# Three edge loops of a four-layer graph network: a PSUM ring of four, and two operations a group later

## What is computed

```
h = relu(layernorm(x));  x += attention over all edges, messages added at the row (layer 0)
h = relu(layernorm(x));  x += edge network (layer 1):
    e    = relu(concat(h[src], edge_attr) @ W1a + b1a) @ W1b + b1b
    agg  = segment_sum(e, dst) / count;   out = relu(concat(h, agg, u) @ W2a + b2a) @ W2b + b2b
h = relu(layernorm(x));  x += GATv2 (layer 2), 4 heads of 64, then 1 head of 128:
    m    = xl[src] + xr[dst] + w_edge * We;   logit = sum(leaky_relu(m) * att)
    out  = segment_sum(segment_softmax(logit) * xl[src], dst)
h = relu(layernorm(x));  x += three EdgeConv steps (layer 3):
    h    = relu([x_i, x_j - x_i] @ W1 + b1) @ W2 + b2;   out = segment_max(h, dst)
```

## Time and profile before

| What | us |
|---|---|
| median of three runs | 12301.65 |
| lowest and highest of them | 12288.66 and 12314.6 |
| the profiled execution, its time | 12306.0 |
| the profiled execution, its span | 12304.2 |

### The profile page before, as it was taken

The page is one execution under the profiler, slowest core; times in us unless marked ns, Lnnn a source line. Parts: engine busy times, 40 slices in busy tenths (PEclk is TensorE's granted clock), DMA queues, the critical chain, the costliest instruction groups (busy, mean ns, idle before and its releaser), DMA issues. The chain is left out here.

```text
span 12304.2 us, 181472 instructions
## 1 busy us (share of the span) xinstructions
PE 7391.4 (60%) x39114; PEld 6245.1 (51%) x39115; DVE 7065.6 (57%) x13587; ACT 2531.9 (21%) x8694; POOL 6720.9 (55%) x6703
## 2 busy tenths in 40 slices
PE   4944444366665677636444443637777677767776
PEld 4944444355554555524344443635555555555554
DVE  6844444433345888866754545675555555555555
ACT  2500000011110000046400000322333233323332
POOL 0088888366642666523236664316666466646665
PEclk7966666555557888879867666768898888888888
DMA  4356556322213666545324443313333334433433
GB/s 118 72 95 96 96 96 97 88 65 65 66 51 93 210 211 213 192 99 157 104 83 127 131 129 103 113 47 129 131 131 132 110 133 132 132 109 132 132 130 121
DMA packets 828886, 1436.26 MB, mean 117 GB/s; under 512 B 183440, under 2 KB 494844, under 8 KB 788336
## 3 DMA queue, kind: packets, MB, share of 16 engines
q1 hardware_dynamic: 531712, 981.94, 25.6%
q0 software_dynamic: 297072, 453.23, 16.7%
HBM read 1115.44 MB, written 320.07 MB: 117 GB/s over the span
## 5 line engine op out<-in xcount | busy, mean ns | idle before, releaser
L1612 POOL DMA_INDIRECT T<-gather_d,srci x2508 | 2516.5, 1003 | 1604.1 <-issue 652.4
L1198 PE MATMUL PS<-T 128*128 x3328 | 1045.0, 404 | 1072.3 <-DVE T L1214 824.1
L838 POOL DMA_INDIRECT added_d<-T,slots x832 | 1292.1, 1553 | 288.4 <-issue 224.1
L920 DVE TENSOR_TENSOR T<-T,PS 128x128 f32 (+1 forms) x2092 | 560.3, 287 | 1465.4 <-remote 1064.7
L1198 PEld LDWEIGHTS PS<-T 128*128 128x128 f32 x3328 | 710.6, 244 | 1223.1 <-issue 1169.7
L1149 POOL DMA_INDIRECT T<-wide_d,srci x832 | 832.6, 1001 | 738.4 <-PEq L71 287.1
L1149 POOL DMA_INDIRECT T<-gather_d,srci x832 | 825.6, 992 | 677.4 <-PEq L71 239.5
L943 POOL DMA_INDIRECT T<-gather_d,srci x832 | 799.8, 961 | 643.3 <-DVE T L1014 265.5
L1731 DVE TENSOR_TENSOR_SCAN T<-T,PS 128x512 f32<-128x512 f32 x624 | 798.1, 1279 | 597.7 <-remote 362.9
L1420 PE MATMUL PS<-T 128*128 128x260 f32 (+1 forms) x3328 | 801.0, 400 | 423.6 <-DVEq L1473 370.0
L1656 PE MATMUL PS<-T,W 128*128 128x512 f32 x1248 | 828.2, 751 | 350.8 <-ACT T L1692 190.2
(11 more groups left out here) (248 smaller groups left out, 14708.2 us busy)
## 6 DMA issues: line engine op xcount, KB each, us to landing
T<-quads_d SPq DMA_DIRECT2D x315, 1024.0 KB
T<-edge_rows_d SPq DMA_DIRECT2D x210, 512.0 KB
edge_rows_d<-T SPq DMA_DIRECT2D x209, 512.0 KB
T<-onehot_t_d SPq DMA_DIRECT2D x416, 256.0 KB
T<-gather_d,srci POOLq DMA_INDIRECT x4172
T<-edge_rows_d SPq DMA_DIRECT2D x210, 256.0 KB
onehot_t_d<-T SPq DMA_DIRECT2D x208, 256.0 KB
edge_rows_d<-T SPq DMA_DIRECT2D x208, 256.0 KB
```

The lines of the kernel that those rows point to most:

```text
L838: gp.indirect_dma_start(added_d[u][:, :], bass.IndirectOffsetOnAxis(ap=slots[:, k:k + 1], axis=0), part(OUT[r], u), None, compute_op=ALU.a ...
L1198: T_.matmul(spot(i, u), part(OT[r], u), T2[:, bass.ds(bs[i * GROUP + u] * width, width)], start=True, stop=False)
L1612: gp.indirect_dma_start(part(R[n % RING], u), None, gather_d[:, :], bass.IndirectOffsetOnAxis(ap=srci[:, k:k + 1], axis=0)).then_inc(rows_ ...
```

## The change

- `edge_logits`: PSUM becomes a ring of four groups. `spot(r, u)` starts at 1024 * r, and PE waits for `logits_in` of group n - 4. The order of instructions stays.
- `edge_mlp_sums`: DVE's order becomes `join(n + 1)`, `hots(n + 2)`, `add(n - 1)`. `hots` gets a wait for `sums_made` of the group four before. The first trip is written out ahead of the loop.
- `edge_maxima`: PE's order becomes `make_products(n)`, `make_edges(n + 1)`, `turn(n - 1)`, `make_ends(n - 3)`. ACT's `turn_out` goes to n - 1. On DVE `add` goes to n - 3 and `mark_ends` to n - 1.
- `LEAD`, the empty steps ahead of the first group, goes from 8 to 16, as DVE reads the block numbers up to three groups back. `STEPS` goes from 848 to 856.

```diff
-LEAD = TURN
+LEAD = 2 * TURN
...
# edge_mlp_sums, vector
                     def hots(n, r):
+                        dve.wait_ge(sums_made.h, sums_made.done(n - RING))
                         V.tensor_tensor(split(O[r]), every(iota[:, :], GROUP), ...
-                    def trip(j, last=False):
+                    def trip(j, first=False, last=False):
...
                             if not (last and r == RING - 1):
                                 join(n + 1, j + (r + 1) // RING, (r + 1) % RING)
-                            add(n, r, bs[r % 2 * GROUP:r % 2 * GROUP + GROUP])
                             if not (last and r >= 2):
                                 hots(n + 2, (r + 2) % RING)
+                            if r or not first:
+                                add(n - 1, (r - 1) % RING, bs[r % 2 * GROUP:r % 2 * GROUP + GROUP])
# edge_logits
-            spot = lambda i, u: PS[:, 2048 * i + u // per_bank * 512 + u % per_bank * width:][:, 0:width]
+            spot = lambda r, u: PS[:, 1024 * r + u // per_bank * 512 + u % per_bank * width:][:, 0:width]
...
-                            pe.wait_ge(logits_in.h, logits_in.done(n - 2))
+                            pe.wait_ge(logits_in.h, logits_in.done(n - RING))
...
-                                last = T_.matmul(spot(i, u), ident[:, :], part(R[r], u, width), start=False, stop=True)
+                                last = T_.matmul(spot(r, u), ident[:, :], part(R[r], u, width), start=False, stop=True)
# edge_maxima, tensor
                             make_products(n, r % 2)
                             make_edges(n + 1, j + (r + 1) // RING, (r + 1) % RING)
-                            make_ends(n - 2, r % 2)
-                            turn(n, r % 2)
+                            turn(n - 1, 1 - r % 2)
+                            make_ends(n - 3, 1 - r % 2)
# edge_maxima, scalar
-                            turn_out(n, r % 2)
+                            turn_out(n - 1, 1 - r % 2)
# edge_maxima, vector
                             scan(n, j, r)
                             make_hots(n + 2, j + (r + 2) // RING, (r + 2) % RING)
-                            add(n - 2, r % 2, bs[r % 2 * GROUP:r % 2 * GROUP + GROUP])
-                            mark_ends(n, r % 2, j * per_trip + (r * GROUP + LEAD))
+                            add(n - 3, 1 - r % 2, bs[r % 2 * GROUP:r % 2 * GROUP + GROUP])
+                            mark_ends(n - 1, 1 - r % 2, j * per_trip + ((r - 1) * GROUP + LEAD))
```

More of the change, by code:

```diff
@@ L1038, in _ @@
                     join(0, 0, 0)
-                    with dve.Fori(0, trips - 1) as j:
-                        c.open(j, per_trip)
+                    trip(0, first=True)
+                    with dve.Fori(1, trips - 1) as j:
+                        c.open(j - 1, per_trip)
                         trip(j)
-                    c.close(trips - 1)
+                    c.close(trips - 2)
                     trip(trips - 1, last=True)
+                    ends = numbers_at(dve, brow, LEAD + (GROUPS - 1) * GROUP, GROUP, BLOCKS)
+                    add(GROUPS - 1, RING - 1, ends)
             for s in (edges_made, sums_made, relued, rows_added, hots_made, added):
@@ L1195, in _ @@
                             pe.wait_ge(tiles_in[r].h, tiles_in[r].at(16 * j + 16))
-                            pe.wait_ge(logits_in.h, logits_in.done(n - 2))
+                            pe.wait_ge(logits_in.h, logits_in.done(n - RING))
                             for u in range(GROUP):
-                                T_.matmul(spot(i, u), part(OT[r], u), T2[:, bass.ds(bs[i * GROUP + u] * width, width)], start=True, stop=False)
+                                T_.matmul(spot(r, u), part(OT[r], u), T2[:, bass.ds(bs[i * GROUP + u] * width, width)], start=True, stop=False)
                                 pe.wait_ge(rows_in[r][u].h, rows_in[r][u].at(16 * j + 16))
-                                last = T_.matmul(spot(i, u), ident[:, :], part(R[r], u, width), start=False, stop=True)
+                                last = T_.matmul(spot(r, u), ident[:, :], part(R[r], u, width), start=False, stop=True)
                             last.then_inc(products_made.h, 1)
@@ L1213, in take @@
                         for u in range(GROUP):
-                            last = V.scalar_tensor_tensor(part(M[r], u, width), we, ew[:, bass.ds(step_of(n) + u, 1)], spot(r % 2, u), ALU.mult, ALU.add)
+                            last = V.scalar_tensor_tensor(part(M[r], u, width), we, ew[:, bass.ds(step_of(n) + u, 1)], spot(r, u), ALU.mult, ALU.add)
                         last.then_inc(logits_in.h, 1)
@@ L1630, in _ @@
                         s.lead(pe)
-                    turned.lead(pe)
-                    ends_made.lead(pe, 2)
+                    turned.lead(pe, 1)
+                    ends_made.lead(pe, 3)
                     def turn(n, i):
@@ L1671, in _ @@
                             make_edges(n + 1, j + (r + 1) // RING, (r + 1) % RING)
-                            make_ends(n - 2, r % 2)
-                            turn(n, r % 2)
+                            turn(n - 1, 1 - r % 2)
+                            make_ends(n - 3, 1 - r % 2)
+                    turn(GROUPS - 1, 1)
+                    make_ends(GROUPS - 3, 1)
                     make_ends(GROUPS - 2, 0)
@@ L1680, in _ @@
                         s.lead(act)
-                    turned_out.lead(act)
+                    turned_out.lead(act, 1)
                     def lay(n, i, bs):
@@ L1720, in _ @@
                     c.link(V.memset(H[:, :], 0.0))
-                    for s in (scanned, end_hots, hots_made):
+                    for s in (scanned, hots_made):
                         s.lead(dve)
-                    added.lead(dve, 2)
+                    end_hots.lead(dve, 1)
+                    added.lead(dve, 3)
                     def scan(n, j, r):
@@ L1755, in _ @@
                             if r % 2 == 0:
-                                bs = numbers_at(dve, brow, j * per_trip + (r * GROUP + LEAD - 2 * GROUP), 2 * GROUP, BLOCKS)
+                                bs = numbers_at(dve, brow, j * per_trip + (r * GROUP + LEAD - 3 * GROUP), 2 * GROUP, BLOCKS)
                             scan(n, j, r)
                             make_hots(n + 2, j + (r + 2) // RING, (r + 2) % RING)
-                            add(n - 2, r % 2, bs[r % 2 * GROUP:r % 2 * GROUP + GROUP])
-                            mark_ends(n, r % 2, j * per_trip + (r * GROUP + LEAD))
+                            add(n - 3, 1 - r % 2, bs[r % 2 * GROUP:r % 2 * GROUP + GROUP])
+                            mark_ends(n - 1, 1 - r % 2, j * per_trip + ((r - 1) * GROUP + LEAD))
                     c.close(trips)
-                    ends = numbers_at(dve, brow, LEAD + (GROUPS - 2) * GROUP, 2 * GROUP, BLOCKS)
-                    add(GROUPS - 2, 0, ends[0:GROUP])
-                    add(GROUPS - 1, 1, ends[GROUP:])
+                    ends = numbers_at(dve, brow, LEAD + (GROUPS - 3) * GROUP, 3 * GROUP, BLOCKS)
+                    add(GROUPS - 3, 1, ends[0:GROUP])
+                    mark_ends(GROUPS - 1, 1, LEAD + (GROUPS - 1) * GROUP)
+                    add(GROUPS - 2, 0, ends[GROUP:2 * GROUP])
+                    add(GROUPS - 1, 1, ends[2 * GROUP:])
             for s in (products_made, scanned, end_hots, turned, ends_made, turned_out, added):
```

3 lines of the change are left out of this document (2 added, 1 removed).

## The result

The changed kernel takes 12183.32 us (median of four runs, 12161.81 to 12191.99) beside 12300.17 us of the kernel before. The ratio is 0.990 with an interval of 0.9885 to 0.9916, which is 1.0% faster, about 117 us. The profiled execution took 12161.81 us with a span of 12160.1, so it is 144 us under the one profiled before.

The account below looks back on a forecast made before the run. It took POOL's gathers with their issue as each stage's floor, with POOL's waits on top. Terms -45 - 95 - 40 - 20 = -200 took 12306.0 to 12106, rounded to 12100 for the median; 8-in-10 range 11880 to 12330.

Parts of the forecast that it names:

- Edge network, -45: Edge network: `join` first after a stop gains 74 us over 67 pauses, less 29 us for PE's later sums: -45.
- The charge of 29 us for PE's path: Edge network: PE's sums go on 0.87 us later after each of 67 pauses, 58 us, half put on the path.
- Wide logits, -95: Wide logits: PSUM ring of four removes PE's wait for `take`, so POOL pauses less: -95, bounds -170 and +33.
- I take half of all: Wide logits: half of the -191 that removing all of POOL's pauses would bring, taken as -95.
- the narrow pattern of 4.2 groups a pause: Wide logits: pausing once in 4.2 groups, as the narrow logits do, instead of 3.2 removes 15 pauses of 3.2 us: -49.
- transfers that crowd each other: Wide logits: crowding transfers could lengthen gathers by another 0.04 us on 830, the upper bound of +33.
- The sign of being right: Wide logits: POOL's waits fall to about 115 us, with PE's wait for `take` all but gone.
- Narrow logits, -40: Narrow logits: PE's freedom brings little, a fifth of POOL's 192.1 us of waits: -40.
- Maxima, -20: Three maxima: PE's wait for the relu replaces that for the scan; 0.03 us for each of 624 groups, rounded to -20.
- Signals held whatever the order: Rival, all loops: PE's signals come only with POOL's stop, so only single microseconds go: 12265 to 12305; chance 0.13.
- Slower by the clock: Rival, wide logits: PE, less busy, drops to 1.2 GHz, +157 for the stage, 12383 in all; chance 0.13 for slower.
- The floor is reached: Rival, all loops: a small gain lets POOL's run go on and the pauses vanish, -657, so 11645; chance 0.13.

## Why the prediction was right or wrong

The forecast was 12100 with a range of 11880 to 12330, and the time is 12183. The sign and the range held. The gain was overstated by 83 us: -200 forecast, -117 measured.

**What bounds the kernel.** Right, and shown more plainly than I could expect: where no signal is late, the loops run at POOL's pace of gathers and issue. So the stops are what the late signals cost, some 150 to 290 us a loop by the lengths on both kinds of chip.

**Edge network, -45.** Right in what ends the pause; -33 in the profile, and -61 to -68 in this loop as a part alone. In the pause shown, the 0.8 us that `join` would lose again was 1.2, and PE's further wait 0.70 instead of 0.87. Over all 67 pauses 52 us went where the working had 74. The charge of 29 us for PE's path is seen in no row. What took its place is a term that the working had at nothing: the gathers grew by 19.4 us. `hots` now runs right behind `join`, and 161 gathers instead of 71 start while it runs; each of these takes 0.21 us more. That -52 + 19 = -33 lies near -74 + 29 = -45 is in part luck.

**Wide logits, -95.** This is the term that was too large. The step that failed is "I take half of all". The row that I had beside it was the better guide: coming to the narrow pattern of 4.2 groups a pause would give -49. Idle time fell by 48.8 us (738.4 to 689.6), and the gathers grew by 17.3: -49 + 17 = -32. I had both sizes among my figures and put neither in the sum. But the cause that I gave for longer gathers, transfers that crowd each other, isn't what the traces show: gathers that start on none of DVE's passes with two SBUF inputs take 0.94 to 0.96 us in this loop, at a DMA share of 0.66, as they do at 0.24. The growth is that of the gathers which start on L1224 (0.29 us more each instead of 0.22). And the agreement with -49 is luck in part. With the ring alone the pauses became fewer and longer, POOL's sum fell by 13 and not by 32, and in the whole the ring also takes back what the edge network's new order costs this loop. The sign of being right that I had named, waits of about 115 us, wasn't reached: they are 163.

**Narrow logits, -40.** -38 in the profile, but +3 as a part alone. It was right once by chance: on another chip the gathers' gain went into longer stops. What was missing in the working is SP. Moving SP's load two groups closer brought 17 us in this loop on one chip, and ring and load together 43 on another; SP's queue held `rows_free_again` behind a wait for PE. I had named the queues that are moved past, but not the one that stayed where it was in POOL's chain.

**Maxima, -20.** Right that one wait takes the place of another: PE's 590.9 us for the scan went, and its waits ahead of the products grew by 705. -13 in the profile, -39 alone. I hadn't seen that the rhythm would change. POOL's pauses went from 375 to 588, that is from one in 6.7 gathers to one in 4.3, and from 577 us in all to 753 (the 468.5 of the earlier trace rows left out those put down to PE). The gathers went from 1003 to 953 ns (-127 us of busy time), mostly since those that start on `mark_ends` were held longer before (in the first loop 131 of them by 0.38 us each, now 96 by 0.07), and the idle time rose by 114. So the -20, a third of 0.09 us for each group, was near by chance.

**The rivals.** "Signals held whatever the order" had more in it than the 0.13 that I gave it: in five loops of these experiments stops and gathers traded places, and the loop stayed. By the Trainium skill ("TensorE: Matmul & The Clock Gate", section "HAM oscillation — how this bites in real kernels") a second PSUM buffer gave a matmul kernel nothing; by that rule the logits would be 0. The ring alone, at 12 us, is near it; with the other parts it was worth about 0.3%. "Slower by the clock" didn't come: the granted clock of the wide stage is 0.86, and was 0.87. Its premise, that a less busy PE shows a lower clock, doesn't fit either: the edge network has 839.68 us busy at 0.50, the narrow logits 595.18 at 0.69. The same page of the Trainium skill, section "A second HAM failure mode: psum-queue depth-cycling", ties a clock that goes to and fro to cycling through PSUM banks with short idle times between bursts; by that rule the ring would at best leave 0.87, and the 0.86 agrees. But on the chip without late signals the wide stage with the same ring of four shows 0.99, so that cycling alone doesn't decide it:

```profile
3645.00:4750.00 1105.00, 824.35 (x3322) 598.57 (x3322) 1059.89 (x1443) 0.00 (x0) 850.62 (x830) 0.99 0.77 246
```

"The floor is reached" didn't happen by this change. On the chip without late signals, the kernel before is within 0.1% of one whose loops are at the floor, so by its time it is there before any change. What the change is worth there was not measured alone; with the load three ahead on top it is that 0.1%.

## What to carry to other kernels

A wait that a change removes is worth what the next wait leaves; where a row beside the estimate shows a pattern that the loop will fall into, price that pattern and its side cost instead of a half. Moving a DVE operation also moves which gathers start while it runs, and this cost or saved as much here as some of the terms of the sum. When an engine in order stores, waits and loads for others, look for a wait in it that belongs to something not needed yet: moving one load by two groups brought 42 us in two loops on one chip, where the PSUM ring alone had brought 12 on another. And late signals were there on some chips and not on another, so a gain that comes from them should be measured on more than one.

## What the runs showed that was not expected

- Late signals of PE are not the same on all chips. The kernel before takes 12300 to 12430 us on those that have them and 11142 on one that has not, with gathers of about the same length. What makes the difference isn't known. A run of gathers alone can't be the cause, as I had read it from one chip, since the same runs hold nothing on the other.
- On the chips with late signals the time of a loop hardly follows the stops' pattern. Maxima loops with runs of four, of eight and of both took 1243 to 1253 us within one set. Fewer gathers, SP's load, the ring and the edge network's order are what made a loop shorter by more. Why stops and gathers trade against one another so closely is open.
- A gather takes longer when it starts while DVE is in a pass with two inputs in SBUF: by what is left of the pass, less 0.13 us. In these rows, from the chip without late signals, 0.43 us of L1224 are left when the second gather starts, and it takes 0.30 more:

```profile
4201.72 0.95 POOL L1154 DMA_INDIRECT T<-wide_d,srci  x1 [0.30 <-issue]
4202.18 1.22 DVE L1224 SCALAR_TENSOR_TENSOR T<-T 128x1024 f32<-128x1024 f32 x1
...
4202.97 1.25 POOL L1154 DMA_INDIRECT T<-wide_d,srci  x1 [0.30 <-issue]
```

  In the wide loop of the changed kernel 196 gathers start on L1224, with 0.41 us of it left on average, and take 0.29 more. The 202 that start near the end of the multiplication (L1225, 0.15 left) take 0.03 more. Those that start on the reduction (L1226, one input) or on `take` (L1219, which reads PSUM) take no longer. The same holds for `hots` in the edge network (0.34 left, 0.21 more). The Trainium skill ("SBUF — State Buffer", section "SBUF: two separate sides") says that a DVE operation with two SBUF inputs which started first has a shared pair of ports for the whole instruction, against POOL operations that read SBUF. These rows agree.
- The loop of the values (L1420, L1425 after) isn't touched by the change, and yet PE's matmuls in it take 384 to 388 ns instead of 397 to 400 in every kernel that has the edge network's new order, in the run with that part alone too, and not in those with the ring alone or the maxima alone:

```profile
L1420 PE MATMUL PS<-T 128*128 128x260 f32 (+1 forms) x3328 | 801.0, 400 | 423.6 <-DVEq L1473 370.0
```

```profile
L1425 PE MATMUL PS<-T 128*128 128x260 f32 (+1 forms) x3328 | 761.7, 385 | 447.7 <-DVEq L1478 391.5
```

  Busy and idle together fall by 15 us (1224.6 to 1209.4). Whether it is where the code lies or when the loop starts was not tried.
- The two kernels that have the edge network's new order and the old PSUM have a longer wide loop, though nothing in it differs (sums of 1612.7 and 1610.0 against 1571.1). In each of them 46 gathers take near 2.0 us, every one of them the first after a stop, and 45 of the 46 started 0.05 to 0.07 us behind the beginning of L1224. With the old order in the edge network (the kernel with the maxima alone) there are 6. That is the 40 us. Why DVE and POOL come out of a stop in another step there isn't known.
